# Cross-attention heads: the last weighting's pieces in another order, and more of the next head's chunks inside it

## The chip, the cores and the metric

The kernel runs on one core of one Trainium2 chip. The metric is device time in microseconds (us) of one execution, on that core. Engines are named as in the profile: PE is TensorE's products, PEld its weight loads, DVE is VectorE, ACT is ScalarE, POOL is GpSimd, SP is SyncE, which issues most transfers.

## The reference, cut to what matters

A decoder layer: self-attention, cross-attention with a residual, and a channel mix. The change lies in the cross-attention, in which all 2048 tokens attend to all 4096 rows of the context, in 8 heads of width 128:

```python
def _L0_xattn_ref(x, context, Wq, Wk, Wv, Wout, bout):
...
    qh = _split_heads(jnp.einsum('bnq,qi->bni', x, Wq))
    kh = _split_heads(jnp.einsum('bmc,ci->bmi', context, Wk))
    vh = _split_heads(jnp.einsum('bmc,ci->bmi', context, Wv))
    sim = jnp.einsum('hid,hjd->hij', qh, kh) * SCALE
    mean = jnp.mean(sim, axis=-1, keepdims=True)
    sim = (sim - mean) * ATTN_MATRIX_SCALE + mean
    attn = jax.nn.softmax(sim, axis=-1)
    out = jnp.einsum('hij,hjd->hid', attn, vh)
...
    return jnp.einsum('bni,iq->bnq', out, Wout) + bout
```

A weighted sum over keys does not depend on the order in which the keys are added, except for rounding.

## The kernel before

For each head the kernel projects keys (4096 columns, in four chunks `K+` of 1024) and values (eight blocks V of 512 keys) from blocks of the context that SyncE loads, two at a time, into four places (`blocks`). Then eight groups of 256 queries pass. Every number is held as a high and a low part, so a product of two is three products: high x high, high x low, low x high.

The work is written as lists of items, and each of PE, ACT and DVE walks the same lists in the same order (`run_heads`, L1416) and does its part of each item. The items that matter here:

- `A t i` (`A+` for the next group): scores of 128 queries (half t of a group) against 1024 keys (chunk i). PE does 6 products of 512 columns (L1638), DVE scales them into `probs` and takes the maximum (L1799).
- `M t`: the maximum over the four chunks (DVE, L1805). `E t i`: the exponential of one chunk (ACT, L1737).
- `V b` (`V+` for the next head): one value block. PE does 12 products of 256 columns (L1621), ACT casts each half to `v_hi` (L1761), DVE makes `v_lo` by four operations (L1852, L1857).
- `Q+`: the projection of the next queries (PE L1630, ACT L1746, DVE L1837). `out`: the output projection of a group, added to x by DVE (L1652, L1829). `O`: rounding of a finished weighting (L1743, L1821).
- `T c` and `W c`: a piece of 256 keys. PE transposes the probabilities (4 transpositions, L1698), ACT and DVE make `pt_hi` (L1731) and `pt_lo` (L1810), and two pieces later PE weighs the values with them (6 products, L1709). A weighting has 16 pieces, in slots 0 to 15; `with_pieces` (L1340) puts the other items behind the pieces of their slots.

All items that PE fills into PSUM outside of pieces (`A`, `V`, `K+`, `Q+`, `out`) are chunks. They share two buffers `s_ps` in turn: PE waits until DVE has freed the chunk two places back:

```python
if kind in IS_CHUNK:
    if items is not BEFORE or n >= 2:
        pe.wait_ge(freed, chunk + (n - 1))
    buf = (chunk_par + n) % 2
```

A head is STEP_0, STEP_1, STEP (five times), STEP_7, STEP_8, AFTER. STEP_1 to STEP_8 hold a weighting each, of the group before; STEP_0 and AFTER hold none. The weighting in STEP_8 is the head's last; in it the next head's last key chunks, first scores and two value blocks are made. A value block b holds the keys of pieces 2b and 2b + 1 and can be overwritten once these are weighed. BEFORE comes once, ahead of the first head. The last head ends with lists of its own (LAST_7, LAST_8), which the change leaves as they are.

SyncE loads blocks 4 to 7 for the next head when K+0 and K+1 have been made, blocks 0 and 1 when V+5 has (which frees their places), blocks 2 and 3 when V+6 has, and the next queries when the ones before are projected.

## Time and profile before

| | us |
|---|---|
| median of 3 runs | 2589.2 |
| lowest and highest | 2586.34 and 2589.95 |
| the profiled execution, its own time | 2587.6 |
| its span | 2585.8 |
| PE busy in the span | 2522.9 |
| DVE, ACT busy | 1914.0, 1607.7 |

The span runs from the first to the last instruction in the profile; the execution's own time has 1.8 us more around it. PE is busy nearly all of it, DVE three quarters, ACT under two thirds. "Busy" of PE counts a product until its modelled end, which lies behind the start of the next one, so the distances between starts tell what work costs.

### The profile page before, as it was taken

What the parts mean: (1) busy time and instruction counts of PE and PEld (TensorE: products, weight loads), DVE (VectorE), ACT (ScalarE), POOL (GpSimd) and SP (SyncE); (2) the same over time, 40 slices, a digit from 0 to 9 for tenths busy, and PEclk for the clock granted to TensorE, in tenths of its full rate; (3) what the DMA queues carried; (4) which work ended last, traced back from release to release, by engine and by line L of the source; (5) the groups of instructions that cost most, each with busy time, mean ns of one, the idle gap of its engine ahead of it and who ended that gap; (6) DMA issues with size and microseconds to landing.
All of it is one profiled execution on the core that took longest, in us unless ns stands there. A gap on an engine that the chain in (4) does not pass through costs nothing. (4 is left out here: it accounts for less than half of the span.)

```text
span 2585.8 us, 47026 instructions
## 1 busy us (share of the span) xinstructions
PE 2522.9 (98%) x17647; PEld 2290.0 (89%) x17647; DVE 1914.0 (74%) x3606; ACT 1607.7 (62%) x3049; POOL 158.2 (6%) x208
## 2 busy tenths in 40 slices
PE   8999979999999999999999999999999999999998
PEld 6899868999899989998999899988999899989987
DVE  5889767777777677777777777777777777677787
ACT  6899646655566555565666565656665566655566
POOL 1344220000000000000000000000000000000003
PEclk9999999999999999999999999999999999999999
DMA  8765350001200120011000300030001200110000
GB/s 247 214 162 147 98 226 28 17 17 58 74 17 16 66 74 17 16 66 66 21 21 9 123 17 17 17 110 30 17 17 58 74 17 16 66 68 17 28 1 33
DMA packets 60637, 155.47 MB, mean 60 GB/s; under 512 B 8848, under 2 KB 22352, under 8 KB 60464
## 3 DMA queue, kind: packets, MB, share of 16 engines
q1 hardware_dynamic: 56464, 140.15, 16.8%
q0 software_dynamic: 3248, 12.72, 1.6%
q8 instruction: 113, 1.85, 0.3%
q14 instruction: 60, 0.49, 0.1%
q10 hardware_dynamic: 752, 0.26, 0.0%
HBM read 125.70 MB, written 27.39 MB: 59 GB/s over the span
## 5 line engine op out<-in xcount | busy, mean ns | idle before, releaser
L1731 ACT CAST pt_hi<-xt_ps 128x512 fp32r<-128x512 f32 x1024 | 592.7, 585 | 566.4 <-PE xt_ps L1698 550.7
L1810 DVE TENSOR_TENSOR pt_lo<-xt_ps,pt_hi 128x512 fp32r<-128x512 f32 x1024 | 704.5, 688 | 253.6 <-ACT pt_hi L1731 248.3
L1799 DVE TENSOR_SCALAR_CACHE_REDUCE xprobs<-xs_ps 128x1024 f32<-128x1024 f32 x512 | 626.5, 1224 | 175.9 <-PE xs_ps L1638 171.4
L1709 PE MATMUL xo_ps<-pt_hi,v_hi 128*128 128x256 f32 x2048 | 647.4, 316 | 2.4 <-DVE pt_lo L1810 2.3
L1737 ACT ACTIVATE xprobs<-xprobs,xneg_max 128x1024 f32<-128x1024 f32 x512 | 591.5, 1155 | 27.2 <-DVE xneg_max L1805 27.2
L1698 PE MATMUL xt_ps<-ident,xprobs 128*128 128x128 f32 x4096 | 602.1, 272 | 0.0
L1709 PE MATMUL xo_ps<-pt_hi,v_lo 128*128 128x256 f32 x2048 | 571.3, 279 | 0.0
L1709 PE MATMUL xo_ps<-pt_lo,v_hi 128*128 128x256 f32 x2048 | 570.1, 278 | 0.0
L1698 PEld LDWEIGHTS xt_ps<-ident,xprobs 128*128 128x128 f32 x4096 | 486.5, 140 | 59.0
L1709 PEld LDWEIGHTS xo_ps<-pt_hi,v_hi 128*128 128x128 f32 x2048 | 386.3, 189 | 5.7 <-DVE pt_lo L1810 2.6
L1709 PEld LDWEIGHTS xo_ps<-pt_lo,v_hi 128*128 128x128 f32 x2048 | 388.3, 190 | 2.0
L1709 PEld LDWEIGHTS xo_ps<-pt_hi,v_lo 128*128 128x128 f32 x2048 | 383.8, 187 | 0.0
L1638 PE MATMUL xs_ps<-k_hi,q_hi 128*128 128x512 f32 x1024 | 330.0, 403 | 5.0 <-DVE v_lo L1857 3.4
L1638 PE MATMUL xs_ps<-k_lo,q_hi 128*128 128x512 f32 x1024 | 321.5, 395 | 0.0
L1638 PE MATMUL xs_ps<-k_hi,q_lo 128*128 128x512 f32 x1024 | 320.8, 394 | 0.0
L1638 PEld LDWEIGHTS xs_ps<-k_hi,q_lo 128*128 128x128 f32 x1024 | 192.0, 187 | 46.9
L1638 PEld LDWEIGHTS xs_ps<-k_lo,q_hi 128*128 128x128 f32 x1024 | 192.0, 187 | 46.5
L1638 PEld LDWEIGHTS xs_ps<-k_hi,q_hi 128*128 128x128 f32 x1024 | 156.5, 188 | 14.4 <-DVE v_lo L1857 9.0
L1583 POOL TENSOR_SCALAR xprobs<-x,wo_raw 128x256 f32<-128x256 f32 x8 | 9.7, 1215 | 2148.1 <-DVE wo_raw L1308 2148.1
L832 ACT ACTIVATE probs<-s_ps,neg_max 128x512 f32<-128x512 f32 (+3 forms) x256 | 120.4, 555 | 1.9 <-DVE neg_max L872 1.9
L880 DVE TENSOR_TENSOR spt_lo<-t_ps,spt_hi 128x512 fp32r<-128x512 f32 x160 | 104.0, 682 | 20.9 <-ACT spt_hi L841 20.8
L1743 ACT CAST v_split<-xo_ps 128x256 fp32r<-128x256 f32 x64 | 23.9, 374 | 147.9 <-PE xo_ps L1709 147.9
(251 smaller groups left out, 2722.6 us busy)
## 6 DMA issues: line engine op xcount, KB each, us to landing
v_split<-ctx_split SPq DMA_DIRECT2D x68, 768.0 KB, 5.9
xq<-x_split SPq DMA_DIRECT2D x64, 512.0 KB, 3.3
q_st<-rel_split SPq DMA_DIRECT2D x32, 256.0 KB, 3.7
q_st<-q_split SPq DMA_DIRECT2D x32, 192.0 KB, 4.4
k_st<-k_split SPq DMA_DIRECT2D x32, 192.0 KB, 4.6
ctx_split<-ctx_out POOLq DMA_DIRECT2D x8, 768.0 KB, 4.0
q_split<-attn_late SPq DMA_DIRECT2D x8, 512.0 KB, 4.0
k_split<-attn_late SPq DMA_DIRECT2D x8, 512.0 KB, 5.5
```

The costliest lines, as they stand in the source:

```text
L832: last = act.activation(probs[:, n % 2, k, TILE_AT[i]:TILE_AT[i] + w], bank[:, c:c + w], ACT.Exp, bias=neg_max[:, n % 2, i, k:k + 1])
L880: dve.tensor_tensor(pt_lo[:, m % 4, :], t_ps[:, m % 3, :], pt_hi[:, m % 4, :].bitcast(F32), ALU.subtract).then_inc(pt_ready, 1)
L1583: pool.tensor_scalar(mix.y[:, t, :], x[:, t, :], mix.mv[:, t, 0:1], mix.rstd[:, t:t + 1], ALU.subtract, ALU.mult).then_inc(mix.pool_done, 1)
L1638: last = pe.matmul(s_ps[:, buf, BLK * b:BLK * (b + 1)], q[:, par, P * t:P * (t + 1)], k[:, k0:k0 + BLK], start=m == 0, stop=m == 2)
L1698: last = pe.transpose(t_ps[:, c % 3, GQ * j + P * t:GQ * j + P * (t + 1)], probs[:, 1 - par, t, P * (2 * c + j):P * (2 * c + j + 1)], iden ...
L1709: last = pe.matmul(o_ps[:, 0:GQ], v[:, vs], pt[:, c % 3, GQ * j:GQ * (j + 1)], start=c == 0 and j == 0 and m == 0, stop=c == PIECES - 1 an ...
L1731: act.copy(pt_hi[:, c % 3, :], t_ps[:, c % 3, :]).then_inc(t_rounded, 1)
L1737: ins = act.activation(probs[:, par, t, cols], probs[:, par, t, cols], ACT.Exp, bias=neg_max[:, par, t:t + 1], accum_out=chunk_sum[:, par, ...
L1743: act.copy(o_hi[:], o_ps[:, 0:GQ]).then_inc(o_rounded, 1)
L1799: dve.tensor_scalar(probs[:, par if kind == "A" else 1 - par, t, CHUNK * i:CHUNK * (i + 1)], s_ps[:, buf, :], LOGIT, None, ALU.mult, ALU.m ...
L1810: dve.tensor_tensor(pt_lo[:, c % 3, :], t_ps[:, c % 3, :], pt_hi[:, c % 3, :].bitcast(F32), ALU.subtract).then_inc(t_ready, 1)
```

## The change

Four things, all in the lists and what they need:

- The weighting of STEP_8 takes its pieces from key columns 2048 to 4095 first and then 0 to 2047 (`keys_of`). So the values of the upper blocks are used up first.
- STEP_8 now also holds Q+, V+7, V+6, V+0, M 0, E(0,0), E(0,1), A(1,0) and A(1,1) of the next head; AFTER holds A+(1,2), A+(1,3), E+(0,2), E+(0,3), V+1 and M+1; STEP_0 keeps E(1,0) to E(1,3), V3, V2 and three score chunks of the next group.
- BEFORE takes up, in an order of its own, what the first head would miss.
- Kinds "Q", "E+" and "M+" are new names of the same operations on the other half of a buffer; V 0 and V 1 became V+ 0 and V+ 1, made ahead of the head they belong to.

```diff
-STEP_0 = [("M", 0), ("A", 1, 1), ("E", 0, 0), ("E", 0, 1), ("V", 1), ("A", 1, 2), ("E", 0, 2), ("V", 0), ("A", 1, 3),
-          ("E", 0, 3), ("M", 1), ("V", 3), ("E", 1, 0), ("Q+",), ("E", 1, 1), ("V", 2), ("A+", 0, 0), ("E", 1, 2),
-          ("A+", 0, 1), ("E", 1, 3), ("A+", 0, 2)]
+STEP_0 = [("E", 1, 0), ("V", 3), ("E", 1, 1), ("A+", 0, 0), ("E", 1, 2), ("V", 2), ("E", 1, 3), ("A+", 0, 1), ("A+", 0, 2)]
...
-STEP_8 = with_pieces({0: [("K+", 2)], 1: [("I",)], 2: [("K+", 3)], 4: [("out",)], 6: [("A", 0, 0)],
-                      8: [("A", 0, 1)], 10: [("A", 0, 2)], 12: [("A", 0, 3)], 13: [("V+", 4)], 15: [("V+", 5)]}, [("O",)])
-AFTER = [("V+", 7), ("O",), ("V+", 6), ("A+", 1, 0), ("out",)]
+STEP_8 = with_pieces({0: [("K+", 2)], 1: [("I",)], 2: [("K+", 3)], 3: [("Q+",)], 4: [("out",)], 5: [("V+", 4)], 6: [("A", 0, 0)],
+                      7: [("V+", 5)], 8: [("A", 0, 1)], 9: [("V+", 7)], 10: [("A", 0, 2)], 11: [("V+", 6)],
+                      12: [("A", 0, 3)], 13: [("M", 0), ("V+", 0)], 14: [("E", 0, 0), ("A", 1, 0)],
+                      15: [("E", 0, 1), ("A", 1, 1)]}, [("O",)])
+AFTER = [("O",), ("A+", 1, 2), ("E+", 0, 2), ("V+", 1), ("E+", 0, 3), ("A+", 1, 3), ("M+", 1), ("out",)]
...
-          ("A+", 0, 3), ("V+", 4), ("V+", 5), ("V+", 7), ("V+", 6), ("A+", 1, 0)]
+          ("A+", 0, 3), ("V+", 4), ("M+", 0), ("E+", 0, 0), ("V+", 5), ("E+", 0, 1), ("V+", 7), ("Q",), ("V+", 6), ("E+", 0, 2),
+          ("A+", 1, 0), ("E+", 0, 3), ("A+", 1, 1), ("V+", 0), ("A+", 1, 2), ("V+", 1), ("A+", 1, 3), ("M+", 1)]
...
-                                                    (STEP_8, ("V+", 5), STEP_AT[G]), (AFTER, ("V+", 6), AFTER_AT))]
+                                                    (STEP_8, ("V+", 5), STEP_AT[G]), (STEP_8, ("V+", 6), STEP_AT[G]))]
...
+            def keys_of(items, c, j):
+
+                piece = (c + PIECES // 2) % PIECES if items is STEP_8 else c
+                return slice(P * (2 * piece + j), P * (2 * piece + j + 1))
```

The lines of the changed kernel are numbered a little higher than those of the one before (L1639 for L1638, L1622 for L1621, L1653 for L1652, L1768 for L1761, L1744 for L1737, L1737 for L1731).

**TensorE, from the end of a head's last weighting.** `xs_ps` from k and q is a score chunk (three rows), from `kv_split` a value block (12 products), from `v_split` alone `out`. Before:

```order
L1621 MATMUL xs_ps<-kv_split,v_split 128x256 x24
L1638 MATMUL xs_ps<-k_hi,q_hi 128x512 x2
L1638 MATMUL xs_ps<-k_lo,q_hi 128x512 x2
L1638 MATMUL xs_ps<-k_hi,q_lo 128x512 x2
L1652 MATMUL xs_ps<-v_split 128x256 x6
L1638 MATMUL xs_ps<-k_hi,q_hi 128x512 x2
L1638 MATMUL xs_ps<-k_lo,q_hi 128x512 x2
L1638 MATMUL xs_ps<-k_hi,q_lo 128x512 x2
L1621 MATMUL xs_ps<-kv_split,v_split 128x256 x12
L1638 MATMUL xs_ps<-k_hi,q_hi 128x512 x2
L1638 MATMUL xs_ps<-k_lo,q_hi 128x512 x2
L1638 MATMUL xs_ps<-k_hi,q_lo 128x512 x2
```
With the change:

```order
L1639 MATMUL xs_ps<-k_hi,q_hi 128x512 x2
L1639 MATMUL xs_ps<-k_lo,q_hi 128x512 x2
L1639 MATMUL xs_ps<-k_hi,q_lo 128x512 x2
L1622 MATMUL xs_ps<-kv_split,v_split 128x256 x12
L1639 MATMUL xs_ps<-k_hi,q_hi 128x512 x2
L1639 MATMUL xs_ps<-k_lo,q_hi 128x512 x2
L1639 MATMUL xs_ps<-k_hi,q_lo 128x512 x2
L1653 MATMUL xs_ps<-v_split 128x256 x6
L1622 MATMUL xs_ps<-kv_split,v_split 128x256 x12
L1639 MATMUL xs_ps<-k_hi,q_hi 128x512 x2
L1639 MATMUL xs_ps<-k_lo,q_hi 128x512 x2
L1639 MATMUL xs_ps<-k_hi,q_lo 128x512 x2
```
Two value blocks and a score chunk have left the beginning; now scores, a value block, scores, `out`, a value block follow each other.

**ScalarE, toward the end of the last weighting.** `pt_hi` is the cast of a piece, `v_hi` are the two casts of a value block, `v_split` is `O`. Before:

```order
L1731 CAST pt_hi<-xt_ps 128x512 x11
L1761 CAST v_hi<-xs_ps 128x256 x2
L1731 CAST pt_hi<-xt_ps 128x512 x2
L1761 CAST v_hi<-xs_ps 128x256 x4
L1743 CAST v_split<-xo_ps 128x256
L1761 CAST v_hi<-xs_ps 128x256 x2
L1737 ACTIVATE xprobs,chunk_sum<-xprobs,xneg_max 128x1024 x2
```
With the change:

```order
L1768 CAST v_hi<-xs_ps 128x256 x2
L1737 CAST pt_hi<-xt_ps 128x512 x2
L1768 CAST v_hi<-xs_ps 128x256 x2
L1737 CAST pt_hi<-xt_ps 128x512 x2
L1768 CAST v_hi<-xs_ps 128x256 x2
L1737 CAST pt_hi<-xt_ps 128x512
L1744 ACTIVATE xprobs,chunk_sum<-xprobs,xneg_max 128x1024
L1737 CAST pt_hi<-xt_ps 128x512
L1744 ACTIVATE xprobs,chunk_sum<-xprobs,xneg_max 128x1024
L1750 CAST v_split<-xo_ps 128x256
L1744 ACTIVATE xprobs,chunk_sum<-xprobs,xneg_max 128x1024
```
Every second piece now has a value block's casts behind it, and two exponentials stand between the last pieces.

**ScalarE, ahead of the first head.** `q_hi` is the cast of queries. Before:

```order
L1761 CAST v_hi<-xs_ps 128x256 x8
L1737 ACT_TABLE_LOAD
L1737 ACTIVATE xprobs,chunk_sum<-xprobs,xneg_max 128x1024 x2
L1761 CAST v_hi<-xs_ps 128x256 x2
L1737 ACTIVATE xprobs,chunk_sum<-xprobs,xneg_max 128x1024
L1761 CAST v_hi<-xs_ps 128x256 x2
L1737 ACTIVATE xprobs,chunk_sum<-xprobs,xneg_max 128x1024
L1761 CAST v_hi<-xs_ps 128x256 x2
L1737 ACTIVATE xprobs,chunk_sum<-xprobs,xneg_max 128x1024
L1746 CAST q_hi<-xs_ps 128x256
```
With the change:

```order
L1768 CAST v_hi<-xs_ps 128x256 x2
L1744 ACT_TABLE_LOAD
L1744 ACTIVATE xprobs,chunk_sum<-xprobs,xneg_max 128x1024
L1768 CAST v_hi<-xs_ps 128x256 x2
L1744 ACTIVATE xprobs,chunk_sum<-xprobs,xneg_max 128x1024
L1768 CAST v_hi<-xs_ps 128x256 x2
L1753 CAST q_hi<-xs_ps 128x256
L1768 CAST v_hi<-xs_ps 128x256 x2
L1744 ACTIVATE xprobs,chunk_sum<-xprobs,xneg_max 128x1024 x2
L1768 CAST v_hi<-xs_ps 128x256 x4
L1744 ACTIVATE xprobs,chunk_sum<-xprobs,xneg_max 128x1024
L1768 CAST v_hi<-xs_ps 128x256 x2
```
The exponentials of the first score half have moved in between value blocks, the table load with them.

## Rows read from the trace of the kernel before

**Rows 1.** The page: busy time of the engines
```profile
PE 2522.9 (98%) x17647; PEld 2290.0 (89%) x17647; DVE 1914.0 (74%) x3606; ACT 1607.7 (62%) x3049; POOL 158.2 (6%) x208
```

**Rows 2.** Windows: start:end, length, busy (xinstructions) of each engine, clock, DMA share, GB/s
```profile
373.19:399.96 26.77, 23.98 (x145) 19.78 (x145) 21.75 (x50) 16.58 (x34) 0.00 (x0) 1.00 0.43 158
...
647.42:671.58 24.16, 21.75 (x128) 17.67 (x127) 18.70 (x44) 13.86 (x30) 0.00 (x0) 1.00 0.49 173
...
671.58:919.35 247.77, 247.69 (x1771) 227.76 (x1770) 179.70 (x331) 147.66 (x269) 0.00 (x0) 1.00 0.09 29
...
2278.11:2302.27 24.16, 21.75 (x129) 17.68 (x128) 18.70 (x44) 13.86 (x30) 0.00 (x0) 1.00 0.42 156
```

**Rows 3.** The waits inside 647.42 to 671.58: us in total, times, longest
```profile
PEld xs_ps L1621 <- DVE v_lo L1857: 2.6, 3, 1.2
```

**Rows 4.** Timeline of TensorE: start, length, line, out<-in, [idle before it <- releaser]
```profile
634.74 0.63 PE L1638 MATMUL xs_ps<-k_hi,q_hi 128*128 128x512 f32 x2
...
636.14 0.60 PE L1698 MATMUL xt_ps<-ident,xprobs 128*128 128x128 f32 x4
...
637.26 0.60 PE L1698 MATMUL xt_ps<-ident,xprobs 128*128 128x128 f32 x4
...
647.42 2.99 PE L1621 MATMUL xs_ps<-kv_split,v_split 128*128 128x256 f32 x24
...
653.51 0.74 PE L1638 MATMUL xs_ps<-k_hi,q_hi 128*128 128x512 f32 x2 [0.16 <-DVE xprobs L1799]
...
655.02 1.57 PE L1621 MATMUL xs_ps<-kv_split,v_split 128*128 128x256 f32 x12
...
658.89 1.68 PE L1621 MATMUL xs_ps<-kv_split,v_split 128*128 128x256 f32 x12 [0.72 <-DVE v_lo L1857]
...
660.40 0.63 PE L1638 MATMUL xs_ps<-k_hi,q_hi 128*128 128x512 f32 x2
```

**Rows 5.** Timeline of VectorE and ScalarE in the same place
```profile
652.24 1.21 DVE L1799 TENSOR_SCALAR_CACHE_REDUCE xprobs<-xs_ps 128x1024 f32<-128x1024 f32 x1
...
654.30 0.16 DVE L1805 TENSOR_REDUCE xneg_max<-chunk_max 128x1 f32<-128x4 f32 x1
...
654.50 1.15 ACT L1737 ACTIVATE xprobs<-xprobs,xneg_max 128x1024 f32<-128x1024 f32 x1 [3.67 <-DVE xneg_max L1805]
...
655.22 1.23 DVE L1799 TENSOR_SCALAR_CACHE_REDUCE xprobs<-xs_ps 128x1024 f32<-128x1024 f32 x1 [0.76 <-PE xs_ps L1638]
...
655.64 1.14 ACT L1737 ACTIVATE xprobs<-xprobs,xneg_max 128x1024 f32<-128x1024 f32 x1
...
657.16 0.42 DVE L1852 TENSOR_TENSOR v_rest<-xs_ps,v_hi 128x256 f32<-128x256 f32 x1 [0.71 <-ACT v_hi L1761]
...
658.75 1.21 DVE L1799 TENSOR_SCALAR_CACHE_REDUCE xprobs<-xs_ps 128x1024 f32<-128x1024 f32 x1
...
659.90 0.37 ACT L1761 CAST v_hi<-xs_ps 128x256 fp32r<-128x256 f32 x1 [1.36 <-PE xs_ps L1621]
...
660.30 0.42 DVE L1852 TENSOR_TENSOR v_rest<-xs_ps,v_hi 128x256 f32<-128x256 f32 x1 [0.33 <-ACT v_hi L1761]
```

**Rows 6.** Timeline of VectorE in the last weighting of a head
```profile
640.01 1.23 DVE L1799 TENSOR_SCALAR_CACHE_REDUCE xprobs<-xs_ps 128x1024 f32<-128x1024 f32 x1 [0.80 <-PE xs_ps L1638]
...
643.81 0.68 DVE L1810 TENSOR_TENSOR pt_lo<-xt_ps,pt_hi 128x512 fp32r<-128x512 f32 x1
```

**Rows 7.** Timeline: SyncE's loads of context blocks and queries, and one wait for them
```profile
376.39 3.96 SPq L935 DMA_DIRECT2D v_split<-ctx_split  x4
...
384.14 1.65 PE L1621 MATMUL xs_ps<-kv_split,v_split 128*128 128x256 f32 x12 [1.48 <-DMA v_split<-ctx_split]
...
614.90 0.34 SPq L1514 DMA_DIRECT2D xq<-x_split  x1
```

**Rows 8.** Timeline of ScalarE around a load of its table
```profile
2511.29 1.28 ACT L1301 ACT_TABLE_LOAD   x1
2512.59 0.21 ACT L1301 ACTIVATE wo_raw<-wo_raw 128x12 f32<-128x12 f32 x1
```

More of the change, by code:

```diff
@@ L1336 @@
 PIECES = KEYS // (2 * P)
-IS_CHUNK = ("A", "A+", "out", "Q+", "K+", "V+", "V", "MT")
+IS_CHUNK = ("A", "A+", "out", "Q", "Q+", "K+", "V+", "V", "MT")
 def with_pieces(extra, ahead=()):
@@ L1498, in cross_attention @@
         block = ctx.enter_context(nc.Block())
-        KV_ORDER = [("K+", i) for i in range(4)] + [("V+", b) for b in (4, 5, 7, 6)] + [("V", b) for b in (1, 0, 3, 2)]
+        KV_ORDER = [("K+", i) for i in range(4)] + [("V+", b) for b in (4, 5, 7, 6, 0, 1)] + [("V", b) for b in (3, 2)]
         def v_half(b, half, bank):
@@ L1608, in project_k, with project_v @@
                 return last
-            def project_v(b, h, buf, items):
+            def project_v(kind, b, h, buf, items):
                 if items is BEFORE and b in (4, 7):
@@ L1615, in project_v @@
                 if b < 4:
-                    pe.wait_ge(blocks_loaded[b // 2], h * 64 + 96)
+                    pe.wait_ge(blocks_loaded[b // 2], (h if kind == "V" else h + 1) * 64 + 96)
                 for t in range(BLK // P):
@@ L1670, in run @@
                             last = scores(item[1], item[2], 1 - par, buf)
-                        elif kind == "Q+":
+                        elif kind in ("Q", "Q+"):
                             if items is BEFORE or items is STEP_7:
                                 pe.wait_ge(wq_w, h + 2)
-                            pe.wait_ge(xq_loaded, s * 16 + 32)
+                            pe.wait_ge(xq_loaded, s * 16 + (32 if kind == "Q+" else 48))
                             last = project_q(buf)
@@ L1686, in run @@
                                 pe.wait_ge(kv_w, h + 2)
-                            last = project_k(item[1], h, buf, items) if kind == "K+" else project_v(item[1], h, buf, items)
+                            last = project_k(item[1], h, buf, items) if kind == "K+" else project_v(kind, item[1], h, buf, items)
                         last.then_inc(filled, 1)
@@ L1698, in run @@
                                 last = pe.transpose(t_ps[:, c % 3, GQ * j + P * t:GQ * j + P * (t + 1)],
-                                                    probs[:, 1 - par, t, P * (2 * c + j):P * (2 * c + j + 1)], ident[:])
+                                                    probs[:, 1 - par, t, keys_of(items, c, j)], ident[:])
                         last.then_inc(turned, 1)
@@ L1706, in run @@
                         for j in range(2):
-                            vs = slice(P * (2 * c + j), P * (2 * c + j + 1))
+                            vs = keys_of(items, c, j)
                             for m, (v, pt) in enumerate(((v_hi, pt_hi), (v_hi, pt_lo), (v_lo, pt_hi))):
@@ L1731, in run @@
                         act.copy(pt_hi[:, c % 3, :], t_ps[:, c % 3, :]).then_inc(t_rounded, 1)
-                    elif kind == "E":
+                    elif kind in ("E", "E+"):
                         t, i = item[1:]
+                        of = par if kind == "E" else 1 - par
                         if i == 0:
-                            act.wait_ge(maxed, s * 2 + (t + 1))
+                            act.wait_ge(maxed, (s if items is not BEFORE else s + 1) * 2 + (t + 1))
                         cols = slice(CHUNK * i, CHUNK * (i + 1))
-                        ins = act.activation(probs[:, par, t, cols], probs[:, par, t, cols], ACT.Exp,
-                                             bias=neg_max[:, par, t:t + 1], accum_out=chunk_sum[:, par, t, i:i + 1])
+                        ins = act.activation(probs[:, of, t, cols], probs[:, of, t, cols], ACT.Exp,
+                                             bias=neg_max[:, of, t:t + 1], accum_out=chunk_sum[:, of, t, i:i + 1])
                         if i == 3:
@@ L1743, in run @@
                         act.copy(o_hi[:], o_ps[:, 0:GQ]).then_inc(o_rounded, 1)
-                    elif kind == "Q+":
+                    elif kind in ("Q", "Q+"):
                         act.wait_ge(filled, chunk + (n + 1))
-                        act.copy(q_hi[:, 1 - par, :], s_ps[:, buf, 0:GQ]).then_inc(q_rounded, 1)
+                        act.copy(q_hi[:, 1 - par if kind == "Q+" else par, :], s_ps[:, buf, 0:GQ]).then_inc(q_rounded, 1)
                     elif kind in ("K+", "V+", "V"):
@@ L1801, in run @@
                                           accum_out=chunk_max[:, t, i:i + 1]).then_inc(freed, 1)
-                    elif kind == "M":
+                    elif kind in ("M", "M+"):
                         t = item[1]
+                        of = par if kind == "M" else 1 - par
                         dve.wait_ge(freed, chunk + n)
-                        dve.tensor_reduce(neg_max[:, par, t:t + 1], chunk_max[:, t, :], AX.X, ALU.max,
+                        dve.tensor_reduce(neg_max[:, of, t:t + 1], chunk_max[:, t, :], AX.X, ALU.max,
                                           negate=True).then_inc(maxed, 1)
@@ L1831, in run @@
                         last.then_inc(freed, 1)
-                    elif kind == "Q+":
-                        dve.wait_ge(q_rounded, s + 2)
+                    elif kind in ("Q", "Q+"):
+                        of = 1 - par if kind == "Q+" else par
+                        dve.wait_ge(q_rounded, s + (2 if kind == "Q+" else 3))
                         for t, done in enumerate((q_ready, freed)):
                             half = slice(P * t, P * (t + 1))
-                            dve.tensor_tensor(q_lo[:, 1 - par, half], s_ps[:, buf, half], q_hi[:, 1 - par, half].bitcast(F32),
+                            dve.tensor_tensor(q_lo[:, of, half], s_ps[:, buf, half], q_hi[:, of, half].bitcast(F32),
                                               ALU.subtract).then_inc(done, 1)
```

## The prediction

> **What bounds the kernel now.** I read the page first: TensorE is busy 98% of the span [rows 1], so only two things can move the time, the work TensorE does and the few places where it stands still. The windows say where it stands still. Between two head changes, 671.58 to 919.35, it is busy 247.69 of 247.77 us: nothing to gain there, and VectorE and ScalarE have slack. From the last product of a head's last weighting (647.42) to the first transposition of the next head's STEP_1 (671.58) it is busy 21.75 of 24.16 us, and in the same kind of stretch ahead of the first head 23.98 of 26.77 [rows 2]; the granted clock is 1.00 in all three. There are seven head changes; the first and the last of them stand in the rows, and all seven last 24.16 us. The waits name the releaser: weight loads of value blocks wait 2.6 us, in three places, for VectorE's v_lo [rows 3], and others like them for v_lo or a score chunk. Each chunk (scores A, a value block V, queries Q, out) fills one of two PSUM buffers, and TensorE may fill a buffer again only when VectorE has emptied it.
>
> The reader should see from the timeline what a chunk costs TensorE. A score chunk amid pieces lasts 1.40 (634.74 to 636.14), a piece (4 transpositions, 6 products) 1.12 (636.14 to 637.26). After a stall the first weights are not preloaded and a chunk costs 1.51, scores (653.51 to 655.02) and values (658.89 to 660.40) alike, so I take 1.40 for a V without a stall too, and half of it, 0.70, for Q and out, which have 6 products where V has 12 [rows 4]. The stretch holds 6 V, 7 A, Q and out: 13 x 1.40 + 2 x 0.70 = 19.6. So **4.6 us of the 24.16 are stalls**, as starts count them (the busy column counts overlapping ends as work, hence its smaller gap).
>
> **The change, part by part.** It adds no product, copy, exponential or transfer per head; it reorders. Seven times, V+7, V+6, V+0 (the block that was V 0), A(1,0), A(1,1) and the second queries go from the stretch into the last weighting. On TensorE they cost the same: 5 x 1.40 + 0.70 = 7.7 us. The pieces' order itself (8 to 15, then 0 to 7) costs nothing: the same 16 pieces from other columns. It lets the value blocks of the upper keys be overwritten early.
>
> What remains between the last weighting's end and STEP_1 is A(1,2), V+1, A(1,3), out, V3, A(0,0), V2, A(0,1), A(0,2): 5 A, 3 V and out, 11.9 us if dense. It won't be dense. I walk the queues with these prices. From a score chunk's start to VectorE's start on it 1.7 (653.51 to 655.22); VectorE to the buffer free 1.27 (652.24 to 653.51) [rows 4, 5]. From a V's start to its first cast 1.0 (658.89 to 659.90), to VectorE 0.4 more (660.30), VectorE's four operations 1.6 (657.16 to 658.75), the buffer free 1.73 after their start (658.89). The maximum to the first exponential 0.2 (654.30 to 654.50), and 1.14 for each exponential (655.64) [rows 4, 5]. Zero is the end of the last product.
> - A(1,2) at 0, VectorE on it 1.6, free 2.9; V+1 at 1.4, VectorE from 2.75, free 4.5; A(1,3) at 2.9 (stall 0.1), VectorE from 4.6, free 5.85.
> - out at 4.5 (stall 0.1), VectorE behind the maximum, free 6.9. V3 at 5.85 (stall 0.6). ScalarE has E(1,0) from 6.05 to 7.2 ahead of V3's casts, so VectorE starts V3 at 7.6, free 9.3. A(0,0) at 7.35.
> - V2 at 9.3 (stall 0.55); ScalarE gives E(1,1) and E(1,2) from 7.9 to 10.2, then V2's casts, VectorE from 10.65, free 12.4. A(0,1) at 10.8, A(0,2) at 12.4 (stall 0.2), and the transposition at 13.9. E(1,3), which it needs, ends at 12.5.
>
> So the stretch takes **13.9**, plus 7.7 inside the weighting, 21.6 against 24.16: 2.6 us a head, 7 x 2.6 = **18.2 us saved**. The ends of this term: nothing, if the stalls only move, and all 4.6 x 7 = 32 us, if TensorE never waits.
>
> For the 7.7 us to cost only TensorE's time, the weighting must stay dense. From slot 5 each of its 11 slots now has a piece and a chunk, two slots taking TensorE 2 x 1.12 + 2 x 1.40 = 5.04 us. For one such pair the trace has VectorE's side: score chunk at 640.01, a piece's pt_lo, a V, and the next pt_lo from 643.81 for 0.68: 4.48 us, waits included, and TensorE had no gap there [rows 6]. It keeps up with 0.56 to spare, for longer than shown. So I cost it at nothing; that cover is the first that would be missed.
>
> Waits past which things were moved: SyncE's loads. Blocks 0 and 1 now follow V+5 at slot 7 and are needed at slot 13, some 13.7 us later; blocks 2 and 3 follow V+6 at slot 11, needed about 17 us later. The slowest such load shown, two pairs from 376.39, let its waiter go at 384.14, 7.75 us [rows 7]. The second queries' load goes out at about 614.90 in the same queue as before, and slot 3 comes after three pieces and two key chunks of the next weighting, over 8 us, also more than those 7.75 us. All hidden.
>
> Ahead of the first head there is no weighting to hide in, and the list is new: exponentials now stand between value blocks. Same prices, zero at V+4 (373.19). M+0 waits behind V+4 on VectorE until 3.1, E(0,0) runs 3.3 to 4.4 ahead of V+5's casts, V+5 is free at 6.55 and holds the queries back; V+6 at 8.4, A(1,1) 11.4, V+0 12.9, V+1 15.9, A(1,3) 17.4, V3 19.0, V2 23.7, A(0,2) 26.8, transposition 28.3. Before it was 26.77 [rows 2]: **1.5 us lost**, between a gain of 2 and a loss of 4 (the early exponentials' 4 x 1.14 in full).
>
> One price there can be disputed. A table load of ScalarE now stands right before E(0,0); it takes 1.28 us and the activation starts 1.30 after the load's start [rows 8], so it ends as the maximum arrives and costs nothing. The Trainium skill, page "ScalarE: Activation LUTs", section "What ACT_TABLE_LOAD costs", adds a drain of about 1380 ns to the load's 1283, 2.66 us in all. By the page the first stretch would be some 1.4 us longer still and the sum 2573.9; the trace has the load's time and no drain behind it, so it does not agree, and I keep 1.30.
>
> Sum: 18.2 - 1.5 = 16.7 us less. The profiled execution took 2587.6 us (span 2585.8), 1.6 under the median of the runs, 2589.2; so 2570.9 on its terms and **2572.5 us** on the median's.
>
> **Rivals.**
> - **The weighting is not quite dense.** Six chunks more, each waiting about 0.2 for VectorE (idle 0.16 at 653.51 [rows 4], and weights not preloaded): 1.3 a head back. For: VectorE near 90% of such a pair. Against: rows 6 themselves. Saves 7 x 1.3 - 1.5 = 7.6: 2581.6 us.
> - **The stretch closes more than my walk says.** Its buffers free up so that no stall is left: 32 - 1.5, 2558.7 us. Against: ScalarE puts E(1,0) to E(1,2) ahead of casts.
> - **The stalls only move.** Every chunk in the stretch still alternates through the same two buffers: 0 - 1.5, 2590.7 us. Against: five of the chunks that stall now lie between pieces.
> - **Slower: VectorE becomes the bound of the weighting.** If it sits through each V from the product's first half on (1.0 + 0.4 + 1.6 = 3.0 us instead of 1.6), a pair takes 4.48 + 1.4 = 5.9 against 5.04; over 5.5 pairs that is 4.7 a head, net +2.1, and 7 x 2.1 + 1.5 = 16: 2605 us. It decides for slower from about 5.5 us a pair. Against: between 640.01 and 644.49 VectorE had other work while the products ran.
>
> **How the numbers follow.** A run of this kernel tells a change from none from about 0.2%, 5.2 us. The forecast has 0.70, its own range 2566 to 2579; a weighting not quite dense 0.12; all stalls closed 0.07; stalls only moved 0.06; VectorE the bound 0.05. Faster by over 5.2 us: 0.70 + 0.12 + 0.07 = 0.89; the same 0.06; slower 0.05. The range for 8 in 10 is 2563 to 2582: the forecast, the first rival and the nearer half of the second.
>
> **What would show it.** Right: the seven stretches from the last weighting's end to the first transposition last about 14 us, with stalls at V3 and V2 for v_lo and xprobs; TensorE has no gap in the last weighting; successive head changes stand 2.6 us closer than now; the first stretch is 1 to 2 us longer. Wrong: waits of TensorE for pt_lo or v_lo inside the last weighting, a wait for exponentials ahead of the first transposition, one for a block of the context at V+0 or V3, or a stretch of 16 us or more.

## The result, and the profile after

| | median, us | lowest to highest | runs |
|---|---|---|---|
| before | 2588.7 | 2586.34 to 2589.95 | 4 |
| with the change | 2570.3 | 2569.52 to 2573.84 | 4 |

The ratio is 0.9932, its 95% interval 0.992 to 0.9944: faster by 18.4 us. The same kernel was run again with the last experiments and gave 2573.46 (6 runs), ratio 0.9945 [0.9933, 0.9957]. The median of all ten runs is 2572.35, where 2572.5 was forecast; that these agree to 0.2 us is chance, as the kernel before alone, measured in four sets, has medians from 2587.17 to 2590.04. The profiled execution of the first four has 2573.84 us of its own and a span of 2572.1: it is the longest of them.

The page's line of the engines, which answers to [rows 1]:

```profile
PE 2520.1 (98%) x17647; PEld 2292.0 (89%) x17647; DVE 1911.9 (74%) x3606; ACT 1609.6 (63%) x3049; POOL 158.0 (6%) x208
```

Every count is the same as before, and TensorE's busy time has hardly changed: no work went away. The windows of the changed kernel tell where the time went (start:end, length, busy of each engine, clock, DMA share, GB/s). The first is the stretch ahead of the first head, then one from the first transposition to the end of the head's last weighting, then the head change, then the part with weightings of the next head:

```profile
374.39:402.81 28.42, 24.07 (x146) 19.73 (x146) 21.89 (x50) 16.28 (x34) 0.00 (x0) 1.00 0.42 148
402.81:657.87 255.06, 255.06 (x1826) 234.71 (x1825) 187.09 (x348) 152.44 (x280) 0.00 (x0) 1.00 0.11 40
657.87:671.83 13.96, 13.12 (x75) 10.42 (x74) 10.95 (x26) 9.42 (x19) 0.00 (x0) 1.00 0.24 73
671.83:926.83 255.00, 255.00 (x1825) 234.65 (x1824) 187.15 (x348) 152.44 (x280) 0.00 (x0) 1.00 0.11 40
```

In the kernel before, the part with weightings of the first head was:

```profile
399.96:647.42 247.46, 247.46 (x1771) 227.68 (x1770) 179.63 (x331) 147.66 (x269) 0.00 (x0) 1.00 0.08 29
```

Against this and [rows 2]: the head change lasts 13.96 us instead of 24.16, all seven times. The part with weightings of the first head has grown from 247.46 to 255.06, by 7.6, and TensorE is busy in all of it. 10.2 less and 7.6 more is 2.6 for this head. (In the next head it is 247.77 and 255.00; why the heads differ is told under the table of the experiments.) Measured from one head's first transposition to the next, the six periods of the trace before have a median of 271.74 us, the six with the change 269.05: **2.7 us a head**. The stretch ahead of the first head takes 28.42 instead of 26.77: **1.65 us lost**. Seven times 2.7 less 1.65 is 17.2, and the starts in the trace say the same: from the value block that begins the first stretch to the last output projection (`out`) ahead of the channel mix it was 2163.94 us and is 2146.72. The spans of the two profiled executions differ by less, 13.7 us: with the change the first stretch begins 1.2 us later, and what follows that last `out` takes 2.3 us more. In both places the granted clock was lower in this execution, which the last section shows.

The waits inside the head change, 657.87 to 671.83, those of TensorE's weight loads (us in total, times, longest):

```profile
PEld xs_ps L1622 <- DVE v_lo L1866: 0.8, 1, 0.8
PEld xs_ps L1622 <- DVE xprobs L1806: 0.6, 1, 0.6
PEld xs_ps L1639 <- DVE v_lo L1866: 0.5, 1, 0.5
PEld xs_ps L1653 <- DVE v_lo L1866: 0.4, 1, 0.4
```

That is 2.3 us in all. Before, the same stretch had 2.6 us for value blocks [rows 3] and these, 4.8 us in all:

```profile
PEld xs_ps L1638 <- DVE v_lo L1857: 1.1, 2, 0.9
PEld xs_ps L1652 <- DVE v_lo L1857: 0.7, 1, 0.7
PEld xs_ps L1638 <- DVE xprobs L1799: 0.4, 1, 0.4
```

No wait of TensorE is listed at all between 615 and 657.8, inside the weighting. The timeline of TensorE in the same head change, one line for each chunk, and the first transposition:

```profile
657.87 0.63 PE L1639 MATMUL xs_ps<-k_hi,q_hi 128*128 128x512 f32 x2
...
659.27 1.58 PE L1622 MATMUL xs_ps<-kv_split,v_split 128*128 128x256 f32 x12
...
660.76 0.73 PE L1639 MATMUL xs_ps<-k_hi,q_hi 128*128 128x512 f32 x2
...
662.34 0.98 PE L1653 MATMUL xs_ps<-v_split 128*128 128x256 f32 x6
...
663.75 1.68 PE L1622 MATMUL xs_ps<-kv_split,v_split 128*128 128x256 f32 x12 [0.43 <-DVE xprobs L1806]
...
665.26 0.63 PE L1639 MATMUL xs_ps<-k_hi,q_hi 128*128 128x512 f32 x2
...
667.18 1.68 PE L1622 MATMUL xs_ps<-kv_split,v_split 128*128 128x256 f32 x12 [0.35 <-DVE v_lo L1866]
...
668.70 0.63 PE L1639 MATMUL xs_ps<-k_hi,q_hi 128*128 128x512 f32 x2
...
670.32 0.74 PE L1639 MATMUL xs_ps<-k_hi,q_hi 128*128 128x512 f32 x2
...
671.83 0.60 PE L1704 MATMUL xt_ps<-ident,xprobs 128*128 128x128 f32 x4
```

The loads past which chunks were moved are hidden, as forecast: no chunk of this head change or of the last weighting from its slot 3 on waits for one. Two pairs of the weighting, each a value block, a piece, a score chunk and a piece, as windows:

```profile
634.93:639.96 5.03, 5.03 (x40) 4.71 (x39) 4.03 (x9) 1.92 (x5) 0.00 (x0) 1.00 0.46 160
639.96:645.00 5.04, 5.04 (x41) 4.72 (x40) 4.04 (x9) 1.93 (x5) 0.00 (x0) 1.00 0.39 157
```

TensorE is full, at the 5.04 us that the prediction took, and VectorE has 4.03 us of work in a pair: 80% of it.

### The profile page after: what moved, and what is told of

Read it like the earlier page. It is cut to its first block and busy times, and to the rows that moved or that the text cites. A ratio compares the mean times of both kernels' runs of the same rounds, so it can differ in the third digit from the quotient of the medians.

```text
span 2572.1 us, 47026 instructions
## 1 busy us (share of the span) xinstructions
PE 2520.1 (98%) x17647; PEld 2292.0 (89%) x17647; DVE 1911.9 (74%) x3606; ACT 1609.6 (63%) x3049; POOL 158.0 (6%) x208
## 5 line engine op out<-in xcount | busy, mean ns | idle before, releaser
L1737 ACT CAST pt_hi<-xt_ps 128x512 fp32r<-128x512 f32 x1024 | 592.2, 585 | 547.8 <-PE xt_ps L1704 529.7
L1744 ACT ACTIVATE xprobs<-xprobs,xneg_max 128x1024 f32<-128x1024 f32 x512 | 591.7, 1156 | 13.4 <-DVE xneg_max L1813 13.4
L1639 PE MATMUL xs_ps<-k_hi,q_hi 128*128 128x512 f32 x1024 | 328.5, 402 | 0.8 <-DVE k_lo L1856 0.2
L1639 PE MATMUL xs_ps<-k_lo,q_hi 128*128 128x512 f32 x1024 | 321.5, 395 | 0.0
L1639 PE MATMUL xs_ps<-k_hi,q_lo 128*128 128x512 f32 x1024 | 320.7, 394 | 0.0
L1639 PEld LDWEIGHTS xs_ps<-k_hi,q_lo 128*128 128x128 f32 x1024 | 191.9, 187 | 47.0
L1639 PEld LDWEIGHTS xs_ps<-k_lo,q_hi 128*128 128x128 f32 x1024 | 192.0, 187 | 46.4
L1639 PEld LDWEIGHTS xs_ps<-k_hi,q_hi 128*128 128x128 f32 x1024 | 156.0, 188 | 6.6 <-DVE v_lo L1866 4.5
```

The source lines that it names most:

```text
L1639: last = pe.matmul(s_ps[:, buf, BLK * b:BLK * (b + 1)], q[:, par, P * t:P * (t + 1)], k[:, k0:k0 + BLK], start=m == 0, stop=m == 2)
L1737: act.copy(pt_hi[:, c % 3, :], t_ps[:, c % 3, :]).then_inc(t_rounded, 1)
L1744: ins = act.activation(probs[:, of, t, cols], probs[:, of, t, cols], ACT.Exp, bias=neg_max[:, of, t:t + 1], accum_out=chunk_sum[:, of, t, ...
```

## The experiments

All are edits of the kernel before or of the changed one, most of them in the lists alone. "Stretch" is the head change, from the last weighting's end to the next first transposition; "period" is the median of the six distances between the first transpositions of successive heads; "first" is the stretch ahead of the first head. "Period net" is explained below the table.

| kernel | median us (runs) | ratio to before [95%] | stretch | period | period net | first |
|---|---|---|---|---|---|---|
| before (trace) | 2588.7 (4) | 1 | 24.16 | 271.74 | 271.66 | 26.77 |
| the change | 2570.3 (4) | 0.9932 [0.992, 0.9944] | 13.96 | 269.05 | 269.03 | 28.42 |
| the change, again | 2573.46 (6) | 0.9945 [0.9933, 0.9957] | 13.95 | 268.97 | 268.97 | 30.85 |
| the order of the pieces alone | 2587.88 (10) | 0.9999 [0.999, 1.0009] | 24.16 | 271.65 | 271.63 | 26.49 |
| order and four value blocks | 2586.38 (10) | 0.9994 [0.9984, 1.0003] | 20.94 | 271.64 | 271.45 | 26.77 |
| queries back in the stretch | 2579.84 (5) | 0.9967 [0.9955, 0.998] | 15.86 | 270.23 | 270.21 | 30.86 |
| short work added on VectorE | 2571.71 (4) | 0.9946 [0.9929, 0.9963] | 13.96 | 269.13 | 269.04 | 28.39 |
| long work added on VectorE | 2584.55 (10) | 0.999 [0.9979, 1.0] | 13.95 | 271.07 | 270.89 | 28.44 |
| V+1 in the weighting too | 2568.98 (4) | 0.992 [0.9903, 0.9937] | 12.37 | 268.92 | 268.86 | 28.40 |
| V3's casts ahead of E(1,0) | 2571.73 (4) | 0.9922 [0.9906, 0.9939] | 13.76 | 269.25 | 268.84 | 26.94 |
| first stretch in another order | 2569.13 (4) | 0.992 [0.9903, 0.9936] | 13.95 | 269.16 | 269.03 | 26.28 |
| one kernel of several moves | 2565.42 (4) | 0.9905 [0.9888, 0.9922] | 10.73 | 268.37 | 268.37 | 27.20 |
| the same, again | 2566.07 (5) | 0.9919 [0.9907, 0.9932] | 10.73 | 268.36 | 268.36 | 27.22 |

Each ratio is against runs of the kernel before made beside it. Their medians were 2588.72 us (4 runs) for the change, 2587.65 (25) for the order alone, the value blocks and the two with added work, 2590.04 (7) for V+1, the casts, the first stretch and the first set of the several moves, and 2587.17 (12) for the two repeats and the queries. So ratios compare better than medians do.

**A wait that the change does not touch.** The last key chunk of the next head (`K+3`, slot 2 of the last weighting) needs a block of the context whose load is issued behind `K+1`. In some heads that load comes late. In the kernel with V3's casts first, first head:

```profile
620.12 2.57 PE L1605 MATMUL xs_ps<-v_split,kv_split 128*128 128x512 f32 x10 [0.34 <-DMA v_split<-ctx_split]
```

From the start of `K+0` (603.88) to that of `K+3` this is 16.24 us; where the load does not hold it, it is 15.73 in every kernel but the one of several moves. The kernel before has it too (15.97 in its second head, 16.08 in its seventh). "Period net" is the same median with each period less what its `K+3` was late; it tells small differences better than the period does, and by it the change is worth 2.6 to 2.7 us a head.

**Which part of the change pays.** First the order of the pieces alone, on the kernel before:

```diff
+            def keys_of(items, c, j):
+
+                piece = (c + PIECES // 2) % PIECES if items is STEP_8 else c
+                return slice(P * (2 * piece + j), P * (2 * piece + j + 1))
...
-                vs = slice(P * (2 * c + j), P * (2 * c + j + 1))
+                vs = keys_of(items, c, j)
```

> The kernel before, with the pieces of the last weighting in the new order and nothing else. Theory (the stalls between a head's last weighting and STEP_1 pay for everything): 0, 2588.7 us, the seven stretches still 24.16 us. Rival (the order itself gives or costs something, by the columns that are read): another time, with a changed distance between the pieces of that weighting.

Nothing moved: ratio 0.9999, stretch 24.16. The same products from other columns cost the same, so the order pays only by what it permits. Next, the order with four value blocks in the weighting, and nothing else of the change:

```diff
+STEP_8 = with_pieces({0: [("K+", 2)], 1: [("I",)], 2: [("K+", 3)], 4: [("out",)], 5: [("V+", 4)], 6: [("A", 0, 0)],
+                      7: [("V+", 5)], 8: [("A", 0, 1)], 9: [("V+", 7)], 10: [("A", 0, 2)], 11: [("V+", 6)],
+                      12: [("A", 0, 3)]}, [("O",)])
+AFTER = [("O",), ("A+", 1, 0), ("out",)]
```

> Only the pieces' order and the value blocks V+7 and V+6 inside the weighting; queries, V 0, V 1, A(1,0), A(1,1) and the exponentials stay where they were before. By the same walk through the queues: the stretch ends 2.73 us of value blocks earlier but A(1,1) still waits for A(1,0)'s buffer, and from there the 18.07 us to the first transposition stay; stretch 2.9 + 18.07 = 21.0 us, 0.4 to 0.5 us a head won, 3 us in all (2585.5). Rival (each chunk that goes inside takes its share of the stalls with it, 2 of 6): a third of the 2.7 us a head, 6 us in all (2582.5).

The stretch came out as expected (20.94) and the time did not: the interval includes 1, and the period is 0.1 us under that of before, 0.2 net, where 0.4 to 0.5 was expected. The key chunk `K+2` of the next head starts at 615.75 in the trace before and the weighting ends at 647.42, 31.67 later; here it is 616.10 and 650.84, 34.74. Two value blocks were expected to add 2 x 1.37 = 2.7 us and added 3.1. In the weighting's window of this kernel the waits have a new line:

```profile
PEld xo_ps L1715 <- DVE pt_lo L1816: 0.2, 1, 0.2
```

With the value blocks moved forward, slots 13 to 15 hold bare pieces, and at the last of them TensorE runs up against `pt_lo`, in all seven heads. So part of what the stretch gave up was taken again inside the weighting. Moving the blocks alone is worth 0.2 us a head at most.

Then the changed kernel with the queries put back in the stretch:

```diff
-                      ... 3: [("Q+",)], 4: [("out",)], 5: [("V+", 4)], 6: [("A", 0, 0)],
+                      ... 4: [("out",)], 5: [("V+", 4)], 6: [("A", 0, 0)],
...
-STEP_0 = [("E", 1, 0), ("V", 3), ("E", 1, 1), ("A+", 0, 0), ("E", 1, 2), ("V", 2), ("E", 1, 3), ("A+", 0, 1), ("A+", 0, 2)]
+STEP_0 = [("E", 1, 0), ("V", 3), ("Q+",), ("E", 1, 1), ("E", 1, 2), ("V", 2), ("A+", 0, 0), ("E", 1, 3), ("A+", 0, 1), ("A+", 0, 2)]
```

> The changed kernel, with the second queries back in STEP_0, between V3 and E(1,1), and the rest as changed. Theory (a chunk between others costs its own time and the stalls that its buffer brings): by the walk V2's casts wait for E(1,1) and E(1,2) behind the queries' cast, A(0,1) for V2; the stretch becomes 16.2 us instead of 13.96, the weighting 0.71 shorter, so 1.5 us a head lost, some 11 us in all: more than half of the change's gain on this one chunk. Rival (stalls are shared evenly over the chunks): a sixth of the 2.7 us, 3 us in all.

It loses 1.2 us a head (period 270.23 against 269.05), and the time rises by 6.4 us against the changed kernel run beside it. The edit does more than its expectation says: A(0,0), which stood between V3 and V2, now stands behind V2, and the queries leave the list ahead of the first head too. So the 1.2 us belong to the queries in that place and order, and not to the queries alone. The chunks of this stretch from V3 on, each by its first products:

```profile
664.23 1.68 PE L1622 MATMUL xs_ps<-kv_split,v_split 128*128 128x256 f32 x12 [0.42 <-DVE xprobs L1806]
665.74 0.86 PE L1631 MATMUL xs_ps<-xq,v_split 128*128 128x256 f32 x6
667.66 1.69 PE L1622 MATMUL xs_ps<-kv_split,v_split 128*128 128x256 f32 x12 [1.05 <-DVE v_lo L1866]
...
671.30 0.73 PE L1639 MATMUL xs_ps<-k_hi,q_hi 128*128 128x512 f32 x2 [0.56 <-DVE v_lo L1866]
```

V2 waits 1.05 us for V3's buffer, where it waited 0.35 with the score chunk between them: the queries give TensorE 0.70 us to do while that buffer is held, a score chunk 1.40. That the value blocks alone gave 0.2 us was measured with the queries still in the stretch. What V+0, the two score chunks and the exponentials are worth was not parted further.

**Is VectorE's room in the weighting real?** The changed kernel with an operation of no use behind every `pt_lo` from slot 5 of the last weighting; n is 3 in one kernel and 6 in the other:

```diff
+                        if items is STEP_8 and c >= 5:
+                            many = ident[:].rearrange("p (o d) -> p o d", o=1).to_broadcast([P, n, P])
+                            dve.tensor_reduce(bout[:, n * c:n * c + n], many, AX.X, ALU.max)
```

> The changed kernel, with one more VectorE operation (a maximum over 384 elements, expected near 0.45 us, of no use to the result) behind each pt_lo from slot 5 of the last weighting on. Theory (VectorE has about 1.0 us to spare in each pair of slots, 4.03 busy of 5.04): a pair becomes 4.9 to 5.0, still covered, at most 3 us more than the changed kernel. Rival (the weighting is dense only by its order, and any delay of VectorE comes through): 11 x 0.45 x 7 = 35 us more.

> The same with 768 elements, expected near 0.85 us. Theory: a pair needs 4.03 + 1.7 = 5.7 against 5.04 of TensorE, 0.7 x 5.5 pairs x 7 = 27 us more than the changed kernel, which makes it slower than the kernel before by about 8 us: the rival of the prediction in which VectorE becomes the bound. If VectorE's waits can't be used, more: up to 11 x 0.85 x 7 = 65 us.

The short operation lasts 0.54 us, two a pair. It cost nothing: stretch 13.96, period net 269.04. A pair of this kernel, which still takes TensorE's 5.03 us:

```profile
635.73:640.76 5.03, 5.03 (x40) 4.71 (x39) 4.87 (x11) 1.92 (x5) 0.00 (x0) 1.00 0.38 154
```

VectorE is busy for 4.87 us of it, 0.84 more than in the changed kernel and not 2 x 0.54, because the next operation starts before the one before it has ended. The long one cost 1.9 us a head net, 13 us in all (the kernel with the short one took 12.8 us less), half of what was expected. VectorE's timeline in the kernel with the long operation:

```profile
636.78 0.68 DVE L1818 TENSOR_TENSOR pt_lo<-xt_ps,pt_hi 128x512 fp32r<-128x512 f32 x1
637.38 0.94 DVE L1822 TENSOR_REDUCE bout<-ident 128x6 f32<-128x768 f32 x1
638.23 1.21 DVE L1806 TENSOR_SCALAR_CACHE_REDUCE xprobs<-xs_ps 128x1024 f32<-128x1024 f32 x1
...
642.42 0.68 DVE L1818 TENSOR_TENSOR pt_lo<-xt_ps,pt_hi 128x512 fp32r<-128x512 f32 x1
```

What follows the long operation starts 0.85 us after it, the price that was expected. From one `pt_lo` to the one a pair later it is 642.42 - 636.78 = 5.64 us, where 5.7 was expected. The price of a pair was right; the sum made from it was not. From the first added operation to the last there are 5 pairs, at 0.6 over the 5.04 that is 3.0 us, and 1.9 were lost. VectorE may come to slot 5 ahead of TensorE and first use up that lead, which would explain the difference; it was not measured by itself. TensorE's waits between 615 and 658 in this kernel, none of which the changed kernel has:

```profile
PEld xo_ps L1715 <- DVE pt_lo L1818: 1.0, 1, 1.0
PE xo_ps L1715 <- DVE pt_lo L1818: 0.8, 1, 0.8
PEld xs_ps L1639 <- DVE v_lo L1869: 0.5, 1, 0.5
PE xs_ps L1639 <- DVE v_lo L1869: 0.3, 1, 0.3
```

This is the rival on the slower side, made by hand: it exists, and eats all but 0.8 of the 2.6 us a head when a pair costs VectorE 5.64 us. The change has 4.0 us of work there, and 4.9 was free.

**More of the same.** V+1 in the weighting too, in slot 14, out of AFTER:

```diff
-                      12: [("A", 0, 3)], 13: [("M", 0), ("V+", 0)], 14: [("E", 0, 0), ("A", 1, 0)],
+                      12: [("A", 0, 3)], 13: [("M", 0), ("V+", 0)], 14: [("E", 0, 0), ("A", 1, 0), ("V+", 1)],
...
-AFTER = [("O",), ("A+", 1, 2), ("E+", 0, 2), ("V+", 1), ("E+", 0, 3), ("A+", 1, 3), ("M+", 1), ("out",)]
+AFTER = [("O",), ("A+", 1, 2), ("E+", 0, 2), ("E+", 0, 3), ("A+", 1, 3), ("M+", 1), ("out",)]
```

> The changed kernel, with V+1 also inside the weighting (slot 14, behind A(1,0)). Theory (what is left of the stretch is set by the chain A(1,3), maximum, E(1,0), V3's casts, not by the number of chunks): the stretch falls by the chunk, from 13.96 to about 12.45, the weighting grows by 1.38, net 0.1 a head, 1 us in all, no difference to be measured. Rival (each chunk inside saves its share of the stalls, 2 us over 8 chunks): 0.25 a head more, 2 us; or slot 14 with two chunks leaves VectorE behind and costs something.

The stretch shortened by 1.59 us (13.96 to 12.37), and the block costs 1.4 in the weighting: 0.13 a head by the periods, 0.17 net. The time agrees, but a difference of 1 us lies inside the scatter of the runs.

**ScalarE ahead of VectorE.** The walk put V3's wait down to E(1,0), which runs first on ScalarE:

```diff
-STEP_0 = [("E", 1, 0), ("V", 3), ("E", 1, 1), ("A+", 0, 0), ("E", 1, 2), ("V", 2), ("E", 1, 3), ("A+", 0, 1), ("A+", 0, 2)]
+STEP_0 = [("V", 3), ("E", 1, 0), ("E", 1, 1), ("A+", 0, 0), ("V", 2), ("E", 1, 2), ("E", 1, 3), ("A+", 0, 1), ("A+", 0, 2)]
```

> The changed kernel, with V3's and V2's casts one place earlier in ScalarE's queue (V3 ahead of E(1,0), V2 ahead of E(1,2)). Theory (V3's stall is set by the free buffer of A(1,3), V2's by VectorE on V3, which waits 0.3 for casts behind E(1,0)): the stretch 13.96 becomes 13.7 to 13.9, 0 to 2 us in all. Rival (the exponentials are the chain that binds): pushing E(1,0) back by 1.8 us delays the first transposition, stretch above 14.3, 3 us or more lost.

The stretch is 0.2 shorter: V2's wait of 0.35 is gone, and the last score chunk has one of 0.15. The period looks no shorter (269.25), but this is the trace in which `K+3` was late in five heads of seven, by 0.3 to 1.2 us; net it is 268.84, 0.2 under the change, so the stretch's gain came through. The rival, that the exponentials bind, is out: E(1,0) was pushed back and the first transposition came no later. The unexpected gain is ahead of the first head: 26.94 us instead of 28.42. There, in the changed kernel, V2 waits long:

```profile
398.16 1.68 PE L1622 MATMUL xs_ps<-kv_split,v_split 128*128 128x256 f32 x12 [1.62 <-DVE v_lo L1866]
```

ScalarE, in the same place of the changed kernel:

```profile
394.90 1.15 ACT L1744 ACTIVATE xprobs<-xprobs,xneg_max 128x1024 f32<-128x1024 f32 x1 [2.49 <-DVE xneg_max L1813]
...
396.05 0.62 ACT L1768 CAST v_hi<-xs_ps 128x256 fp32r<-128x256 f32 x2
```

V3's products begin at 393.46, so its first half can be cast from 394.46 (1.0 later, the latency of the prediction); E(1,0) came late to its place ahead of it, and the casts start at 396.05, 1.6 us late. In the head change the same E(1,0) starts at 663.92 and the casts at 665.07, where they could at 664.75: 0.3 late. So the one edit is worth 1.5 in one place and 0.2 in the other, and the rows point to how late the maximum comes.

**The loss ahead of the first head.** BEFORE in an order without exponentials among the first value blocks:

```diff
-          ("A+", 0, 3), ("V+", 4), ("M+", 0), ("E+", 0, 0), ("V+", 5), ("E+", 0, 1), ("V+", 7), ("Q",), ("V+", 6), ("E+", 0, 2),
-          ("A+", 1, 0), ("E+", 0, 3), ("A+", 1, 1), ("V+", 0), ("A+", 1, 2), ("V+", 1), ("A+", 1, 3), ("M+", 1)]
+          ("A+", 0, 3), ("V+", 4), ("V+", 5), ("V+", 7), ("V+", 6), ("A+", 1, 0), ("M+", 0), ("A+", 1, 1), ("E+", 0, 0), ("E+", 0, 1),
+          ("V+", 0), ("A+", 1, 2), ("E+", 0, 2), ("V+", 1), ("A+", 1, 3), ("E+", 0, 3), ("M+", 1), ("Q",)]
```

> The changed kernel, with the list ahead of the first head in an order like the old one (four value blocks together, exponentials later, queries last). Theory (of 28.42 us there, 1.65 more than before, the early exponentials ahead of casts are the cause): 26.8 to 27.2 us, 1.2 to 1.6 us won in the trace, below what the times can tell. Rival (the longer list itself is the cause): 28.4 stays.

26.28 us, 2.14 less than with the change and 0.5 less than before it, and the stretches stay at 13.95. The longer list itself is not the cause of the loss. Two edits each take nearly all of it back or more, this one and the casts ahead of E(1,0) in STEP_0, so it lies in where exponentials stand among casts; this list moves the queries and a score chunk too, and what each move is worth was not parted.

**A version that beats both.** The moves that the walk and the runs recommend, in one kernel: score chunks from slot 1 on, V+1 inside and V3 and the first exponentials of the second half in AFTER, with the first stretch in the order above, to which V3 and these exponentials are added (its list, the order of the value blocks and the exponentials' wait for the maximum are not shown):

```diff
+STEP_8 = with_pieces({0: [("K+", 2)], 1: [("I",), ("A", 0, 0)], 2: [("K+", 3)], 3: [("Q+",), ("A", 0, 1)], 4: [("out",)],
+                      5: [("V+", 4)], 6: [("A", 0, 2)], 7: [("V+", 5)], 8: [("A", 0, 3)], 9: [("M", 0), ("V+", 7)],
+                      10: [("E", 0, 0), ("A", 1, 0)], 11: [("E", 0, 1), ("V+", 6)], 12: [("E", 0, 2), ("A", 1, 1)],
+                      13: [("E", 0, 3), ("V+", 0)], 14: [("A", 1, 2)], 15: [("V+", 1)]}, [("O",)])
+AFTER = [("O",), ("A+", 1, 3), ("M+", 1), ("V+", 3), ("E+", 1, 0), ("out",), ("E+", 1, 1)]
...
+STEP_0 = [("A+", 0, 0), ("E", 1, 2), ("V", 2), ("E", 1, 3), ("A+", 0, 1), ("A+", 0, 2)]
```

> A version meant to be better: A(0,0) to A(1,2) earlier in the last weighting, V+1 in its slot 15, V3 already in AFTER ahead of E(1,0), first list as in e_first_stretch. By the same walk the stretch from the last product to the first transposition takes 10.8 us with two chunks fewer (2.76 us), so 13.56 against 13.96: 0.4 a head, 2.8 in all, and 1.4 ahead of the first head: 2566 us, 4 us less than the changed kernel. If VectorE is late in the fuller slots, nothing or a loss.

> The better version once more: 4 to 6 us less than after_again (2565), by 0.65 us a head and 1.2 us ahead of the first head, as its first trace showed.

10.73 us for the stretch (10.8 expected), no wait of TensorE inside the weighting, and 2565.4 and 2566.1 us: 7.4 us under the changed kernel where both were run side by side (2573.46), and 24.6 and 21.1 under the kernel before beside it. By the traces it is 7 x 0.66 + 1.2 = 5.8 us under the change. Periods of 268.35 to 268.37, all twelve, are the most even of any kernel here. Its score chunk in slot 1 stands ahead of `K+3`, which now starts 17.14 us behind `K+0` instead of 15.73, and in none of its fourteen heads does it wait for its load. Dense, the stretch would be 6 x 1.40 + 0.70 = 9.1; TensorE's weight loads still wait there for 1.4 us in all:

```profile
PEld xs_ps L1639 <- DVE v_lo L1866: 1.4, 2, 1.0
```

**The change once more**, beside these, for the comparison just made and for its own scatter:

> The changed kernel once more, on the chip and beside the runs of e_best_again, to compare the two: 2570 us, a head change every 269.0 us, first stretch 28.4 us. Its first profile had TensorE's granted clock at 0.72 in two stretches of the channel mix; if that belongs to the change, it shows here again, if it differs from one execution to the next, it may not.

Stretch and period repeat (13.95, 268.97), and the first stretch does not: 30.85 us, where 28.42 was measured. The section on the hardware has the reason.

## Why the prediction was right

- **What bounds it.** TensorE had nothing to gain but its stalls. Right: counts and busy time stayed, the time went from waits. Of the 4.6 us of stalls that starts showed in a stretch, 13.96 - 11.9 = 2.1 are left; 2.5 went.
- **The walk of the stretch.** Starts after the end of the last product, forecast and measured: V+1 1.4 and 1.40, A(1,3) 2.9 and 2.89, out 4.5 and 4.47, V3 5.85 and 5.88, A(0,0) 7.35 and 7.39, V2 9.3 and 9.31, A(0,1) 10.8 and 10.83, A(0,2) 12.4 and 12.45, transposition 13.9 and 13.96. A walk of two buffers through three engines with prices from one place of the trace holds to 0.06 us over 14. Its reason for V3's late release, casts behind E(1,0), is borne out: with the casts put first V2's wait of 0.35 went.
- **The chunks inside the weighting.** 7.7 us forecast; the part with weightings grew by 7.6 in the first head. Amid pieces a value block costs 1.36 to 1.37 us rather than the 1.40 that was taken for it, which is most of the step from 2.6 to 2.7 us a head.
- **The cover.** VectorE keeps up: no wait in the weighting. Two numbers of this step were off, both on the careful side. The 0.56 us to spare was read from a pair with its waits counted in; without them VectorE has 4.03 us of work, and 0.84 us more cost nothing. And "slower from about 5.5 us a pair" is too early: at 5.64 the kernel is still no slower than before (ratio 0.999, interval up to 1.0). It is a cover that goes, at two operations of 0.85 us more a pair; whether it is the first was not tried against others.
- **The first stretch.** Forecast Q at 6.55, V6 8.4, V3 19.0, V2 23.7, transposition 28.3; measured 6.56, 8.23, 19.07, 23.77, 28.42, so the loss is 1.65 where 1.5 was said.
- **The table load.** In the changed kernel it stands where the prediction has it:

```profile
376.39 1.28 ACT L1744 ACT_TABLE_LOAD   x1
377.69 1.15 ACT L1744 ACTIVATE xprobs<-xprobs,xneg_max 128x1024 f32<-128x1024 f32 x1
```

  The exponential starts 1.30 us after the load does. The Trainium skill, page "ScalarE: Activation LUTs", section "What ACT_TABLE_LOAD costs", adds a drain of about 1380 ns to the load, 2.66 us in all, which as an estimate would put the exponential at 379.05; the trace has none here either, and the measurement decides.
- **The rivals.** "Not quite dense" and "VectorE the bound" are excluded by the empty list of waits and by the two pads. "Stalls only move" is excluded by the periods, though the kernel with the value blocks alone is just that: a stretch 3.2 us shorter, and 0.2 a head won. The change escapes it; that this is because score chunks and exponentials fill the last slots, and the queries leave the stretch, fits the traces but was not parted. "All closed" was too much by the 2.1 us a head that remain.
- **The sum.** 18.2 - 1.5 = 16.7 forecast, 7 x 2.7 - 1.65 = 17.2 by the trace. The medians say 18.4 and, in the second set, 13.7 against 2587.17; the scatter of the runs is as large as what lies between, so that the median came within 2.2 us of the forecast is in part luck. The terms of the sum, each within 0.7 us of its own measure, are not.

## What to carry to other kernels

When an engine is full but for a stretch in which chunks alternate between two buffers, price each chunk in the stretch against its price in dense work, and try first those that hold a buffer long for little work, such as a half-size projection. Before filling a dense stretch, add up the second engine's work for one pair of slots, and look also at the slots that are emptied by the move: bare ones stalled here. Compare periods only after looking for a wait, such as that for a load, which the change does not touch. A walk of the queues, with each latency taken from one place in the trace, was good to 0.1 us in the head change and 0.2 in the first stretch.
